# First stage of an attention and mixture-of-experts layer: another order of loads, normalising and turning

## What is computed

```python
x = L0_attn_x
xn = _layernorm(x, axis=-1)
x = x + _L0_attn_ref(xn, ...) + _L0_ffn_ref(xn, ...)

# _L0_ffn_ref: a shared expert, a gate, and the best 3 of 7 routed experts
output = silu(x @ Ws1) * (x @ Wsg) @ Ws2
probas = softmax(x @ gate_w + gate_b)
topk of (probas + biases), weights renormalised over the chosen
output += expert_e(x) * w_e     # for each of the 7 experts
```

## Time and profile before

| | |
|---|---|
| median of 3 runs | 1306.52 us (1306.41 to 1306.58) |
| profiled execution | 1306.28 us, its span 1304.4 us |
| busy share of the span | TensorE 98%, VectorE 55%, ScalarE 50%, GpSimd 48% |
| granted TensorE clock | 1.0, mean of the span |

### The profile page before, as it was taken

How to read it: one execution, slowest core, us unless ns; L and a number is a source line. 1 busy time by engine, 2 the same in 40 slices (tenths; PEclk the granted TensorE clock), 3 DMA queues, 4 the chain that set the end, 5 groups by cost and what they waited for, 6 DMA issues and landing times.

```text
span 1304.4 us, 20533 instructions
## 1 busy us (share of the span) xinstructions
PE 1279.4 (98%) x6233; PEld 1047.0 (80%) x6233; DVE 722.1 (55%) x1349; ACT 648.6 (50%) x1163; POOL 626.0 (48%) x535
## 2 busy tenths in 40 slices
PE   4999999999999999999999999999999999999998
PEld 3788898888888888888887688887888888887886
DVE  6472255223222222222224788888888888888777
ACT  6411133222222222222225677777777777777775
POOL 5125566995060003300001577677667777676543
PEclk9999999999999999999999999999999999999999
DMA  9226564664251113311112243322243223323012
GB/s 299 66 98 230 212 221 122 191 183 151 66 154 58 60 55 105 109 62 58 58 49 86 75 97 66 63 47 60 48 79 50 51 54 66 63 37 67 18 50 98
DMA packets 82168, 123.34 MB, mean 95 GB/s; under 512 B 20177, under 2 KB 28497, under 8 KB 82065
## 3 DMA queue, kind: packets, MB, share of 16 engines
q1 hardware_dynamic: 48912, 56.43, 15.5%
q0 software_dynamic: 11312, 27.23, 9.6%
q10 hardware_dynamic: 21840, 38.36, 9.1%
HBM read 74.41 MB, written 39.05 MB: 87 GB/s over the span
## 4 chain that ended last, share of the span: by engine, by line
PE 92%; POOL 2%; DVE 2%; issue 1%; DMA 1%; ACT 1%; SPq 0%; ACTq 0%; POOLq 0%; DVEq 0%
PE bank L49 86%; PE bank L1505 2%; PE bank L1446 2%; PE bank L1588 1%; DMA rot_sin<-sum_b 0%; DMA rows_a<-in_x 0%; POOL sum_b L614 0%; POOL rot_sin L583 0%; POOL slots L493 0%; POOL sum_b L611 0%; POOL rstd L488 0%; POOL rot L588 0%; POOL sum_b L616 0%; SPq L435 0%; DVE stats L945 0%
## 5 line engine op out<-in xcount | busy, mean ns | idle before, releaser
L49 PE MATMUL bank<-store_b,store_a 128*128 128x512 f32 (+1 forms) x1536 | 319.1, 359 | 3.2 <-issue 1.2
L49 PE MATMUL bank<-slots,x_turned 128*128 x1296 | 317.6, 394 | 0.3 <-DVE x_turned L969 0.3
L49 PEld LDWEIGHTS bank<-store_b,store_a 128*128 128x128 f32 x1536 | 256.1, 189 | 60.3 <-issue 8.7
L49 PEld LDWEIGHTS bank<-slots,x_turned 128*128 128x128 f32 x1296 | 239.2, 188 | 48.1 <-issue 0.7
L991 DVE TENSOR_TENSOR hid_t<-bank,hid_t 128x512 fp32r<-128x512 f32 x70 | 48.4, 691 | 342.2 <-ACT hid_t L682 342.2
L49 PE MATMUL bank<-slots,hid_t 128*128 (+1 forms) x840 | 208.4, 397 | 0.0
L49 PE MATMUL bank<-store_b 128*128 128x512 f32 x768 | 180.1, 390 | 0.1
L49 PEld LDWEIGHTS bank<-slots,hid_t 128*128 128x128 f32 x840 | 153.7, 188 | 30.9 <-DVE hid_t L991 0.2
L49 PEld LDWEIGHTS bank<-store_b 128*128 128x128 f32 x768 | 143.8, 188 | 31.1 <-issue 0.9
L1342 DVE TENSOR_TENSOR store_b<-p_store,store_b 128x512 fp32r<-128x512 f32 x128 | 137.0, 1073 | 26.9 <-ACT store_b L863 26.8
L676 ACT ACTIVATE hidden<-bank 128x512 f32<-128x512 f32 x70 | 41.8, 597 | 208.3 <-PE bank L49 208.3
(11 more groups left out here) (200 smaller groups left out, 1767.7 us busy)
## 6 DMA issues: line engine op xcount, KB each, us to landing
staging<-in_w SPq DMA_DIRECT2D x56, 256.0 KB, 2.8
sorted_y<-y_store ACTq DMA_DIRECT2D x54, 256.0 KB, 2.0
rows<-sorted_x ACTq DMA_DIRECT2D x51, 260.0 KB, 2.7
rot_sin<-sum_b SPq DMA_DIRECT2D x128, 64.0 KB, 2.0
staging<-in_wg SPq DMA_DIRECT2D x28, 256.0 KB, 2.8
y_store<-in_x ACTq DMA_DIRECT2D x16, 256.0 KB, 3.4
shared_y<-y_store ACTq DMA_DIRECT2D x16, 256.0 KB, 2.2
raw<-in_wot SPq DMA_DIRECT2D x16, 256.0 KB, 2.8
```

Of the source, the lines that this page charges most:

```text
L49: made = pe.matmul(out, a, b, start=first and n == 0, stop=last and n == len(pairs) - 1, skip_group_check=onto)
```

## The change

Five things are changed, all in the first stage. VectorE normalises tiles 0 to 3 (a new `normalise(t)` in vector_program: subtract the mean, multiply by rstd), and shift_of(0) and shift_of(1) go. TensorE turns only tiles 0 and 1 ahead of up(0), and tiles 2 and 3 behind it. ScalarE's list loses four normalises, its copies of tiles 2 and 3 stand behind split_high(7), and the copy of the gate's weights stands ahead of split_high(6). GpSimd makes rstd_of(1) ahead of shared_low(3). SP asks for chunks 4 and 5 ahead of tile 8's rows, and so on down to tile 11.

```diff
--- sync_program
             for k in range(NS):
                 load_shared(k)
-            for k in range(NS, CH):
+            load_shared(4)
+            load_shared(5)
+            load_x(8)
+            load_shared(6)
+            load_x(9)
+            load_shared(7)
+            load_x(10)
+            load_x(11)
+            for k in range(8, CH):
+                load_shared(k)
                 load_x(k + NT - CH)
-                load_shared(k)
--- pool_program
             shared_low(2)
+            rstd_of(1)
             shared_low(3)
-            rstd_of(1)
--- scalar_program
             def normalise(t):
-                act.wait_ge(on["shift_made"], t // 2 + 1)
+                act.wait_ge(on["shift_made"], t // 2 - 1)
...
             split_high(3, slot1)
-            normalise(0)
-            normalise(1)
             turn_high(0)
             turn_high(1)
             act.dma_start(consts[:], table).then_inc(on["consts_in"], 16)
             split_high(4, slot1)
-            normalise(2)
-            normalise(3)
             split_high(5, slot1)
-            turn_high(2)
-            turn_high(3)
+            act.wait_ge(on["gate_in"], 48)
+            act.activation(gw[:, :, 0:8], gw_raw[:], ACT.Copy).then_inc(on["gw_high"], 1)
             split_high(6, slot1)
             normalise(4)
             normalise(5)
             split_high(7, slot1)
+            turn_high(2)
+            turn_high(3)
             normalise(6)
             normalise(7)
-            act.wait_ge(on["gate_in"], 48)
-            act.activation(gw[:, :, 0:8], gw_raw[:], ACT.Copy).then_inc(on["gw_high"], 1)
--- vector_program
+            def normalise(t):
+
+                dve.wait_ge(on["rstd_ready"], t // 2 + 1)
+                x = row_of(t)[:, 0:D]
+                dve.tensor_scalar(x, x, mv[:, t, 0:1], rstd[:, t:t + 1], ALU.subtract, ALU.mult).then_inc(
+                    on["xn_done"], 1)
...
             statistics(0)
-            shift_of(0)
+            normalise(0)
+            normalise(1)
             statistics(1)
+            turn_low(0)
             statistics(2)
-            turn_low(0)
-            shift_of(1)
             turn_low(1)
+            normalise(2)
+            normalise(3)
             statistics(3)
             shift_of(2)
--- tensor_program
-            for t in range(FIRST_TURNS):
-                turn_rows(t)
+            turn_rows(0)
+            turn_rows(1)
             for b in range(NBK):
...
                 up(b)
+                if b == 0:
+                    turn_rows(2)
+                    turn_rows(3)
```

More of the change, by code:

```diff
@@ L264, in program @@
              "ratio_made", "part_done", "rescaled", "out_done", "out_added")
-        FIRST_TURNS = 4
         TURNS = {0: ((4, 5), (6, 7)), 1: ((8, 9), (10, 11)), 2: ((12, 13), (14, 15))}
```

## The result

| | median | runs |
|---|---|---|
| before | 1306.34 us | 10 runs, 1305.68 to 1307.46 |
| after | 1309.93 us | 10 runs, 1308.31 to 1310.49 |

The ratio is 1.0025, with a 95% interval of 1.0016 to 1.0035. By the medians the change costs 3.6 us; the interval says 2.1 to 4.6. The profiled execution took 1309.08 us, its span 1307.3, 2.9 more than the span of before.

What follows compares the result with a forecast made beforehand. TensorE, busy for 98% of the span, was taken to bound the kernel. An up(1) 1.8 us later added to the profiled 1306.28 gives 1308.1; with 0.24 for the median, 1308.3 us, range 1305.6 to 1310.5.

Steps and rivals of the forecast that it cites:

- case A: First stage: TensorE keeps its pace over 4.6 us of idling; 1308.3 us, 1307.3 to 1309.1; chance 0.40.
- B: TensorE falls back to the slow pace behind the idling, gated(0) ends later; + 0.9 to + 2.7, 1309.2 to 1311.0 us; chance 0.27.
- (1): Tiles 0 and 1 on VectorE: normalises take turns with GpSimd, ending at 10.85 and 12.3; 0.5 us gained for tile 0.
- (2): VectorE's statistics(1) follows the normalises, done at 14.0; GpSimd's shared_low(3) ends at 16.05 instead of 13.02.
- (3): TensorE's up(0) starts at 14.7 instead of 18.85, 4.1 us earlier; slow pace about 3.3 us, ending at about 18.9.
- (4): VectorE's list up to shift_of(2) at 21.6; TensorE turns tiles 2 and 3 and is done at 20.3.
- (5): ScalarE waits for shift_of(2), normalises from 21.65 to 23.15; high copies follow split_high(7), 23.6 to 24.7.
- the chief step: ScalarE's two high copies of tiles 2 and 3 come behind split_high(7), at 23.6 to 24.7.
- (6): TensorE turns tile 4 at 24.9 instead of 22.42 as its bank is full; idle 4.6 us; gated(0) from 25.95 to 28.7.
- (7): Turns of tiles 6 and 7: tile 6 at 29.15, up(1) at 32.1 instead of 30.29, 1.8 us later.
- the one in which normalise neither waits for GpSimd nor makes it wait: VectorE's 128x512 normalise runs without turn-taking; - 0.6 to + 0.6 us, 1306.0 to 1307.1; chance 0.17.
- The faster one: shift_of(2) by 17 lets high copies wait only for chunk 7; tile 4 turned at 20.4, 2.8 us sooner, 1303.7; chance 0.07.

Runs made afterwards that it cites:

- the busy hole: Changed kernel plus 14 unused 128x512 products between the turns of tiles 3 and 4: 1309.21 us, ratio 1.0024 to before; with three scatters in flight 1309.28 us.
- the early copies with three scatters in flight: Changed kernel with high copies of tiles 2 and 3 moved ahead of normalise(4), and three scatters in flight instead of two: 1306.34 us, ratio 0.9996 to before.
- the kernel with the turns alone: Kernel before with only TensorE's list changed, tiles 2 and 3 turned behind up(0): 1309.85 us, ratio 1.0026 to before.
- the one with the loads alone: Kernel before with only SP's new order of chunks and rows: 1308.17 us, ratio 1.0001 to before.

## Why the prediction was right, and where it was not

The forecast was 1308.3 us within 1305.6 to 1310.5, and the time is 1309.93: slower, inside the range, at 1.6 us from the middle case. The chain that makes the loss was foreseen, but its size was not: + 1.8 us was forecast and 3.6 measured, above the 1309.1 at which the forecast case A ends. The number is inside the range because that reached into B. Step by step:

(1) and (2), the turn-taking of VectorE's normalise with GpSimd: right. Tile 0 could be turned at 10.60 (10.85 predicted), both normalises ended at 11.95 (12.3), statistics(1) at 13.6 (14.0), shared_low(3) near 15.6 (16.05). The unknown price of the 128x512 form, taken as 0.43 us, is 0.5 by the pair of 1.00 with GpSimd idle.

(3) up(0) started at 14.28 (14.7). Its pace was mis-sized: I gave the slow pace 3.3 us, and all twelve products had it, 5.49 us in all. up(0) ended at 19.77 and not 18.9. By my own terms it should have read 19.1: 3.3 us at 0.46 us a product leave five of the twelve for the full pace of 0.23. This made the hole shorter and nothing else.

(4) and (5): right within 0.7 us in every row. shift_of(2) at 20.99 (21.6), normalise(4) at 21.19 (21.65), the high copies at 23.13 (23.6), behind split_high(7), as the chief step said. That this place on ScalarE is the cause was shown by moving it: the loss went.

(6) **The step that failed**: "TensorE keeps its pace over the 4.6 us of idling". The hole was 3.64 us and the clock fell; gated(0) took 5.01 us where 2.99 is full pace, the turns ahead of it 1.94 for 1.23. My second case, B, had this at a chance of 0.27 and 1309.2 to 1311.0 us; gated(0) is over its 3.5 us, and the time fell into it. The Trainium skill, "TensorE: Matmul & The Clock Gate", Part 1, says that an idle array falls back to its lower clock; the trace agrees, 0.54 granted over the 7 us behind the hole. I had weighed the hole of 3.78 us before up(0) as no evidence for want of a fast engine ahead of it, and the one of 1.15 as evidence against, which it was not: it is much shorter.

(7) Tile 6 at 31.02 (29.15), up(1) at 33.74 (32.1): + 3.45 us for + 1.8. By the profiles the difference of 1.65 is the clock's: with the stretch kept busy by other products up(1) came at 32.26, near the forecast, 1.5 to 2.1 us sooner.

"I see nothing further on that gives it back" was incomplete. It held for the change itself, whose 3.45 us at up(1) are 2.9 at the end of the span. But in the profiles of two versions that start sooner TensorE waits for GpSimd at the first routed block, by 0.82 and 1.95 us, and this bound I hadn't looked for.

Of the rivals, the one in which normalise neither waits for GpSimd nor makes it wait fell by 2.90 against 1.00 us. The faster one fell at shift_of(2), 20.99 where it needed 17; its split_high(7) would by its own terms have stood at 18.0 and not 18.6. None of my cases said that the high copies' place alone would decide whether the kernel falls behind the time before.

Not settled: how much of the end time the clock's fall costs, and so whether B is why the time came out where it did. The profiles say 1.5 to 2 us at up(1). The ratios to before with and without the fall are 1.0025 and 1.0024, and with three in flight 1.0017 and 1.0019. A profile is one execution; with the same stage it ends up to 2 us from the median, and in four of the ten runs of the changed kernel the mean clock was 0.999 and not 0.997. Both kernels with the busy hole have up(1) only 1.4 to 2.0 us later than the 30.29 of before, and yet their medians are 2.3 us above the kernel before and 3.0 above the kernel before with three in flight; what makes the rest is open too.

## What to carry to other kernels

Feeding TensorE earlier gains nothing if what comes second isn't earlier too: here a start 4.6 us sooner became a hole, and behind the hole TensorE worked at its lower clock. When a step is moved on one engine, go through the lists of the engines behind it and look for a consumer that now stands behind something later; moving two calls on ScalarE was worth the whole loss. And look for the next place at which an engine off the critical path meets it, but test whether it costs anything: here a wait of 1.95 us in one profile was no loss in the medians.

## What was not expected of the hardware

- The hole's length alone doesn't tell whether the clock falls. With 1.91 us of idling behind the turns of tile 3 it stayed (gated(0) 2.98 us), and so it did with 1.96 in the early copies with three scatters in flight (2.98); with the same 1.96 in the kernel with the turns alone it fell for a while (gated(0) 4.03, clock 0.59 from 24 to 27.5 us); with 1.95 near 210 us it fell (4.61 us for twelve products that otherwise take 3.00).
- The granted clock of a stretch can stand as 1.00 where the pace is slow: from 8 to 20 us of both kernels, with up(0) at 5.49 us for twelve products in the changed one and eight transposes at 1.97 in the one before. The duration of a known operation is the better witness at the start of a program.
- A 128x512 normalise with two scalars per row takes 0.5 us on VectorE (1.00 for two), less than ScalarE's 0.76 (1.52 for two), but 1.45 beside GpSimd's subtractions (2.90 for two).
- Four 256 KB chunks, two of them asked for ahead of all of SP's rows, land in 3.9 us (median) in the changed kernel and in 5.1 in the one with the loads alone; each asked for behind a tile's rows, in 7.0.
- With three indirect scatters in flight GpSimd issues all 48 in 68 to 69 us, with two in 85 to 89. In one kernel of five ScalarE then started an operation 5.5 us late (13.05 for 7.6) and TensorE idled 7.46 us; that the scatters are the cause wasn't shown.
